# A four-layer attention and feed-forward kernel: three job tables reordered, one table load moved, 16-bit reads in the last layer's quantiser

## The reference, cut to what matters

```
x = x + L0_xattn(layernorm(x), ctx)      # cross attention, 8 heads of 64          "l0x"
x = x + L0_ffn(layernorm(x))             # causal attention, 16 heads of 64 ("l0f"), then 31 + 1 experts ("l0m")
x = x + L1_xattn(layernorm(x), ctx)      # cross attention, 16 heads of 8          "l1x"
x = x + L1_ffn(layernorm(x))             # causal attention, 16 heads of 8 ("l1f"), then 8 experts ("l1m")
x = x + L2_xattn(...);  x = x + L2_ffn(...)                # "l2x", "l2m"
x = x + L3_xattn(...);  x = x + L3_ffn(layernorm(x))       # "l3x", "l3m"
```

```
x    = act_qdq(x)                          # scale = max|x| / 32767; round, clip, times scale
up   = act_qdq(x @ w_up.T);  gate = act_qdq(x @ w_gate.T)
sig  = fixed_qdq_u16(sigmoid(gate))        # steps of 1/65536
gate = act_qdq(gate * sig);  o = act_qdq(gate * up);  return o @ w_down.T
```

## Time and profile before

| | |
|---|---|
| median of 3 runs | 1324.61 us (1323.27 to 1331.3) |
| the profiled execution | 1321.66 us, its span 1319.8 us |
| granted TensorE clock, mean over the span | 0.961 of full speed |
| PE busy | 1160.2 us, 88% of the span |
| DVE busy | 995.9 us, 75% |
| ACT busy | 875.7 us, 66% |
| POOL busy | 560.5 us, 42% |
| the chain that ended last | PE 59%, ACT 17%, DVE 14%, issue 7% |
| ACT exponentials L1096 on that chain | 13% |

### The profile page before, as it was taken

One profiled execution on the slowest core, in us unless ns is written; L12 is line 12 of the kernel. 1 busy time (PEld: TensorE's weight loads), 2 busy tenths in 40 slices (PEclk: granted clock), 3 DMA queues, 4 the chain that ended last, 5 costly groups with the idle time before them and its releaser, 6 DMA issues.

```text
span 1319.8 us, 29320 instructions
## 1 busy us (share of the span) xinstructions
PE 1160.2 (88%) x10082; PEld 894.7 (68%) x10082; DVE 995.9 (75%) x2234; ACT 875.7 (66%) x2403; POOL 560.5 (42%) x670
## 2 busy tenths in 40 slices
PE   7889889999988999997888899988999989997815
PEld 4677777788766788885666677766788666666403
DVE  6676677667758899997777766767666787887787
ACT  4666466656654799995888777764566447775684
POOL 5710366766653222255222231132877417881100
PEclk8999999999998999997999999998999899998967
DMA  5230000000002556650000010003222028750001
GB/s 168 60 93 16 20 2 2 2 3 2 2 2 87 181 210 212 209 208 1 2 2 2 3 42 2 2 2 114 88 88 84 0 55 206 190 139 1 1 0 33
DMA packets 38865, 83.71 MB, mean 63 GB/s; under 512 B 6066, under 2 KB 19762, under 8 KB 38740
## 3 DMA queue, kind: packets, MB, share of 16 engines
q1 hardware_dynamic: 38740, 82.07, 20.2%
HBM read 80.40 MB, written 1.64 MB: 62 GB/s over the span
## 4 chain that ended last, share of the span: by engine, by line
PE 59%; ACT 17%; DVE 14%; issue 7%; POOL 2%; DMA 1%; ACTq 0%; SPq 0%; POOLq 0%; DVEq 0%
PE score_bank L1662 18%; ACT h_all L1096 13%; PE f_bank L1696 6%; PE score_bank L1521 6%; PE f_bank L1422 4%; PE turn_bank L1537 4%; PE turn_bank L1696 3%; PE out_bank L1696 3%; PE out_bank L1577 2%; PE out_bank L1546 2%; DVE top_score L2006 2%; PE f_bank L1447 1%; DVE work L2018 1%; PE f_bank L1454 1%; DVE part_max L2404 1%
## 5 line engine op out<-in xcount | busy, mean ns | idle before, releaser
L1096 ACT ACTIVATE h_all<-score_bank,top_score 128x128 f32<-128x128 f32 x896 | 276.6, 400 | 101.3 <-DVE top_score L2006 101.2
L1662 PE MATMUL score_bank<-parts 128*128 128x512 f32 x1040 | 296.4, 403 | 9.8 <-DVE h_parts L2212 6.6
L1662 PEld LDWEIGHTS score_bank<-parts 128*128 128x128 f32 x1040 | 191.9, 190 | 75.2 <-DVE h_parts L2212 19.0
L2006 DVE TENSOR_REDUCE top_score<-score_bank 128x4 f32<-128x512 f32 x224 | 143.1, 681 | 105.2 <-PE score_bank L1521 105.2
L2212 DVE TENSOR_TENSOR h_parts<-score_bank,h_parts 128x512 fp32r<-128x512 f32 x260 | 178.3, 686 | 2.7 <-ACT h_parts L1211 2.4
L1211 ACT ACTIVATE h_parts<-score_bank 128x512 fp32r<-128x512 f32 x260 | 155.5, 598 | 31.8 <-PE f_bank L1696 8.5
L778 POOL TENSOR_TENSOR small<-small,half_neg 128x4 f32<-128x4 f32 (+4 forms) x24 | 36.6, 1528 | 177.0 <-DVE small L1981 83.2
L1537 PE MATMUL turn_bank<-CF,h_all 128*128 128x128 f32 x512 | 81.7, 283 | 30.3 <-DVE work L2018 19.0
L1537 PEld LDWEIGHTS turn_bank<-CF,h_all 128*128 128x128 f32 x512 | 56.1, 142 | 57.1 <-POOL h_all L803 18.1
L1188 ACT ACTIVATE score_bank<-score_bank,wset 128x512 f32<-128x512 f32 x128 | 84.6, 662 | 11.8 <-PE score_bank L1662 7.0
L2184 DVE TENSOR_TENSOR score_bank<-work,score_bank 128x512 f32<-128x512 f32 x124 | 86.3, 696 | 8.2 <-ACT score_bank L1188 5.6
(11 more groups left out here) (417 smaller groups left out, 2623.6 us busy)
## 6 DMA issues: line engine op xcount, KB each, us to landing
work<-gates_l0m SPq DMA_DIRECT2D x62, 512.0 KB, 3.9
W0X<-gates_l2m SPq DMA_DIRECT2D x32, 256.0 KB, 3.9
CTX<-gates_l2m SPq DMA_DIRECT2D x32, 256.0 KB, 3.9
wset<-in_l0m SPq DMA_DIRECT2D x32, 128.5 KB, 3.6
W0X<-gates_l1m SPq DMA_DIRECT2D x8, 512.0 KB, 3.8
wset<-in_l1m SPq DMA_DIRECT2D x8, 384.0 KB, 4.6
CTX<-gates_l1m SPq DMA_DIRECT2D x6, 512.0 KB, 4.0
big<-in_w0f SPq DMA_DIRECT2D x4, 512.0 KB, 3.9
```

Of the source, the lines that this page charges most:

```text
L1096: last = act.activation(held[c][:, P * m:P * m + P], score_bank[c][:, P * m:P * m + P], ACT.Exp, bias=top_score[c][:, m:m + 1], **sums)
L1662: last = pe_.matmul(bk[:, :], wt, y[:, x], start=(part == 0), stop=(part == len(parts_of) - 1))
L2006: dve.tensor_reduce(top_score[c][:, :], split(score_bank[c][:, :], HEADS), AX_X, ALU.max, negate=True)\
```

## The change

1. In l0x, DVE's C0 of the last batch goes ahead of N0 of the own batch.
2. In l1x and l1f, three jobs each are moved one place back: on ACT SP goes behind E1, on PE OB goes behind T1, on DVE OB goes behind C1.
3. In S of the causal stages the matmul of two columns (L1498) is taken out, 32 in all.
4. In l3m, `gate_steps` and `other` are taken out, six instructions each. The sigmoid, the product with the sigmoid and the final product now read the low 16 bits of the rounded float32 values in place, through a view as int16 with a stride of two (`steps_in`). The order of roundings, copies and sigmoids on ACT changes with that.
5. A sigmoid of one column ahead of l3m's first wait on ACT makes the table load come there.
6. One POOL wait at the start of l1f uses l1x's number of front jobs in its count instead of l1f's, and the memset of `less_magic` goes.

```diff
@@ ORDER, one line of each list as an example
-        DVE=[("M", 0, "own"), ("M", 1, "own"), ("CS", 0, "next"), ("OP", 0, "before"), ("N", 0, "own"), ("C", 0, "last"), ("C", 1, "last"),
+        DVE=[("M", 0, "own"), ("M", 1, "own"), ("CS", 0, "next"), ("OP", 0, "before"), ("C", 0, "last"), ("N", 0, "own"),
...
-        ACT=[("F", 0, "next"), ("E", 0, "own"), ("SP", 0, "last"), ("E", 1, "own"), ("E", 2, "own"), ("E", 3, "own"),
+        ACT=[("F", 0, "next"), ("E", 0, "own"), ("E", 1, "own"), ("SP", 0, "last"), ("E", 2, "own"), ("E", 3, "own"),
...
+        def steps_in(t, at):
+
+            h = HIDDEN_ORDER[at]
+            return t[:, 1024 * h:1024 * h + 1024].bitcast(I16).rearrange("p (n two) -> p n two", two=2)[:, :, 0]
...
-                                r, k = place(front_at["l1x"], L["front"], PAIRS - 1, s, 0)
+                                r, k = place(front_at["l1x"], LAYERS[2]["front"], PAIRS - 1, s, 0)
...
-            pool.memset(less_magic[:, :], -MAGIC)
...
+            act.activation(prob_rec[0][:, 0:1], top_score[0][:, 0:1], ACT.Sigmoid)
+
             act.wait_ge(step("l3m.scale"), 1)
...
             def sigmoid(at):
-                act.wait_ge(step("l3m.g"), at + 1)
+                act.wait_ge(step("l3m.g_round"), at + 1)
                 if at >= 2:
                     act.wait_ge(step("l3m.gs"), at - 1)
-                act.activation(sig[at % 2][:, :], piece(big, at), ACT.Sigmoid, scale=quant[:, 2, 2:3]).then_inc(step("l3m.sig"), 1)
-
-            def other(at):
-
-                act.wait_ge(step("l3m.u_round"), at + 1)
-                act.activation(piece(U, at), piece(U, at), ACT.Identity, bias=less_magic[:, :]).then_inc(step("l3m.u"), 1)
+                act.activation(sig[at % 2][:, :], steps_in(big, at), ACT.Sigmoid, scale=quant[:, 2, 2:3]).then_inc(step("l3m.sig"), 1)
...
                 rounded(big, at, 2, "l3m.g_round")
-                if at < 3:
-                    copies(0, at + 1)
-                if at == 4:
-                    act.wait_ge(step("l3m.scale"), 3)
-                if at >= 4:
-                    rounded(U, at - 4, 1, "l3m.u_round")
+                if 0 < at < 4:
+                    copies(0, at)
                 sigmoid(at)
-            for at in range(2, 6):
+            act.wait_ge(step("l3m.scale"), 3)
+            for at in range(3):
                 rounded(U, at, 1, "l3m.u_round")
-            for at in range(2):
-                other(at)
             act.wait_ge(step("l3m.scale"), 4)
             for at in range(6):
                 rounded(big, at, 3, "l3m.round3")
-                if 1 <= at <= 4:
-                    other(at + 1)
+                if at < 3:
+                    rounded(U, at + 3, 1, "l3m.u_round")
...
                         if causal:
-
-                            pe_.matmul(banks[0][:, 0:2], ident_bf, own_bf[:, 0:2], start=True, stop=True, skip_group_check=True)
...
-            def gate_steps(at):
-                dve.wait_ge(step("l3m.g_round"), at + 1)
-                dve.tensor_scalar(piece(big, at), piece(big, at), MAGIC, None, ALU.subtract).then_inc(step("l3m.g"), 1)
-
             def by_sigmoid(at):
...
-                dve.scalar_tensor_tensor(piece(big, at), sg, MAGIC / 65536.0, piece(big, at), ALU.subtract, ALU.mult)\
+                dve.scalar_tensor_tensor(piece(big, at), sg, MAGIC / 65536.0, steps_in(big, at), ALU.subtract, ALU.mult)\
...
             chunk_max(0, 0)
-            gate_steps(0)
-            chunk_max(0, 1)
             for at in range(6):
-                if at < 5:
-                    gate_steps(at + 1)
                 last = by_sigmoid(at)
-                if at < 2:
-                    others = chunk_max(0, at + 2)
-                if at == 1:
+                if at < 3:
+                    others = chunk_max(0, at + 1)
+                if at == 2:
                     join_max(others, 1, slice(0, 12))
-                if at == 2:
+                if at == 3:
                     scale(1, 2)
...
-                dve.wait_ge(step("l3m.u"), at + 1)
-                dve.scalar_tensor_tensor(piece(big, at), piece(big, at), MAGIC, piece(work, at), ALU.subtract, ALU.mult)\
+                dve.wait_ge(step("l3m.u_round"), at + 1)
+                dve.scalar_tensor_tensor(piece(big, at), piece(big, at), MAGIC, steps_in(work, at), ALU.subtract, ALU.mult)\
```

More of the change, by code:

```diff
@@ L15 @@
 U8 = mybir.dt.uint8
+I16 = mybir.dt.int16
 P = 128
@@ L54 @@
              ("F", 3, "next")],
-        DVE=[("M", 0, "own"), ("M", 1, "own"), ("CS", 0, "next"), ("OP", 0, "before"), ("N", 0, "own"), ("C", 0, "last"), ("C", 1, "last"),
-             ("N", 1, "own"), ("Y", 0, "after")],
+        DVE=[("M", 0, "own"), ("M", 1, "own"), ("CS", 0, "next"), ("OP", 0, "before"), ("C", 0, "last"), ("N", 0, "own"),
+             ("C", 1, "last"), ("N", 1, "own"), ("Y", 0, "after")],
         POOL=[]),
@@ L70 @@
         PE=[("S", 0, "own"), ("OP", 0, "before"), ("F", 1, "next"), ("V", 0, "last"), ("V", 1, "last"), ("V", 2, "last"),
-            ("V", 3, "last"), ("F", 2, "next"), ("T", 0, "own"), ("OB", 0, "last"), ("T", 1, "own"), ("F", 3, "next"),
+            ("V", 3, "last"), ("F", 2, "next"), ("T", 0, "own"), ("T", 1, "own"), ("OB", 0, "last"), ("F", 3, "next"),
             ("F", 0, "after"), ("T", 2, "own"), ("OT", 0, "last"), ("T", 3, "own")],
-        ACT=[("F", 0, "next"), ("E", 0, "own"), ("SP", 0, "last"), ("E", 1, "own"), ("F", 1, "next"), ("E", 2, "own"),
+        ACT=[("F", 0, "next"), ("E", 0, "own"), ("E", 1, "own"), ("SP", 0, "last"), ("F", 1, "next"), ("E", 2, "own"),
              ("E", 3, "own"), ("F", 3, "next"), ("OT", 0, "last"), ("C", 3, "own")],
         DVE=[("M", 0, "own"), ("OP", 0, "before"), ("M", 1, "own"), ("M", 2, "own"), ("M", 3, "own"), ("F", 2, "next"),
-             ("C", 0, "own"), ("OB", 0, "last"), ("C", 1, "own"), ("C", 2, "own")],
+             ("C", 0, "own"), ("C", 1, "own"), ("OB", 0, "last"), ("C", 2, "own")],
         POOL=[("Y", 0, "after")]),
@@ L79 @@
         PE=[("S", 0, "own"), ("OP", 0, "before"), ("F", 1, "next"), ("V", 0, "last"), ("V", 1, "last"), ("V", 2, "last"),
-            ("V", 3, "last"), ("F", 2, "next"), ("T", 0, "own"), ("OB", 0, "last"), ("T", 1, "own"),
+            ("V", 3, "last"), ("F", 2, "next"), ("T", 0, "own"), ("T", 1, "own"), ("OB", 0, "last"),
             ("F", 0, "after"), ("T", 2, "own"), ("OT", 0, "last"), ("T", 3, "own")],
-        ACT=[("F", 0, "next"), ("E", 0, "own"), ("SP", 0, "last"), ("E", 1, "own"), ("E", 2, "own"), ("E", 3, "own"),
+        ACT=[("F", 0, "next"), ("E", 0, "own"), ("E", 1, "own"), ("SP", 0, "last"), ("E", 2, "own"), ("E", 3, "own"),
              ("C", 2, "own"), ("OT", 0, "last"), ("C", 3, "own")],
         DVE=[("M", 0, "own"), ("OP", 0, "before"), ("M", 1, "own"), ("M", 2, "own"), ("M", 3, "own"), ("F", 1, "next"),
-             ("C", 0, "own"), ("OB", 0, "last"), ("F", 2, "next"), ("C", 1, "own")],
+             ("C", 0, "own"), ("C", 1, "own"), ("OB", 0, "last"), ("F", 2, "next")],
         POOL=[("Y", 0, "after")]),
@@ L269, in build @@
         quant = sb("quant", [P, 6, 4])
-        less_magic = sb("less_magic", [P, 1])
         part_max = sb("part_max", [P, 24])
```

## The result

The changed kernel took 1311.68 us (median of 11 runs, 1308.70 to 1316.98), the kernel before 1323.27 (11 runs of that series, 1321.90 to 1331.30): a ratio of 0.9905, 95% interval 0.9888 to 0.9923. That is 11.6 us by medians; the forecast was 1309 us, range 1303 to 1316. The profiled execution took 1309.09 us with a span of 1307.3, 12.5 us less than before's 1319.8. The prediction had 15.2 us. The interval of the ratio lies on both sides of 0.99, so a gain of over 1%, to which the prediction gave 0.60, is neither shown nor excluded; a gain as such is clear.

The account below looks back on a forecast made before the run. No engine was full; a chain of waits bound the kernel. Terms 5.3 + 3.0 + 1.3 + 5.2 + 0.4 = 15.2 us off the profiled 1321.66 gave 1306.5, plus 2.95 to the median, 1309 us; range 1303 to 1316.

Parts of the forecast that it names:

- the two orders with the matmul: Heads of 8 rows: 5.3 us in l1f and 3.0 in l1x from the orders, 1.3 from the matmul.
- the first case: Whole kernel: everything goes as reckoned, 1306 to 1312 us; chance 0.56.
- The exponentials ahead of SP: l1x and l1f on ACT: E1 ahead of SP removes ACT's wait, 0.35 us per l1f batch, 0.23 per l1x batch.
- The two-column matmul: S on PE: removing it gives 0.09 us per l1f batch, 1.3 us for 15 batches; nothing taken in l0f.
- the first reading: l1f on PE: without the two columns the mask matmuls start 0.58 us behind T3 instead of 0.67.
- rival 2: PE's tiling-mode drain decides: removing the matmul costs 0.05 us in all 32 places, total 1312.3 us; chance 0.13.
- rival 3: l1x and l1f: OB becomes what T3 waits for, eating up to all 8.3 us, 1311 to 1317.7; chance 0.15.
- l3m: Last layer: DVE's unbroken stretch lasts 24.24 us and the joined maximum ends at 1279.7, not 1284.87: 5.2 us gained.
- Rivals 4 and 5: l3m's strided 16-bit reads slow: half rate, 1322.0 us, chance 0.05; or a third of the rate, 1335, chance 0.03.
- the whole phase moves as it is: l3m's final products: ACT's roundings keep ahead of DVE by 0.1 us a piece, so phase and output keep their length.
- l0x: C0 ahead of N0: +0.9 beside POOL's cast, +0.6 at the join, -1.1 one step later; 0.4 us, between -3 and +2.

Follow-up runs that it names:

- e1: The kernel before with only the changed l1x and l1f orders on ACT, PE and DVE, two-column matmul kept; ratio to before 0.9936.
- e8: The kernel before with only ScalarE's order changed in l1x and l1f; one execution, span 1313.7 us, l1f 8.00 and l1x 8.07 us a batch.
- e9: The kernel before with only the PE and DVE orders changed in l1x and l1f; one execution, span 1327.2 us.
- e2: The kernel before with only l3m's gate part changed (16-bit reads, no subtractions), table load left with the first sigmoid; ratio 0.9963.
- e6: The changed kernel without its early one-column sigmoid, so the table loads at the first real sigmoid; 1309.50 us, ratio to before 0.9885.
- e4: The changed kernel with DVE's old order kept for the last step of l0x; 1306.74 us, ratio to before 0.9867.
- e12: The changed kernel with DVE's old order in the last step of l0x, run a second time; 1308.30 us, ratio to before 0.9873.
- e11: The changed kernel a third time, no edit; one execution, span 1306.7 us.
- e10: The changed kernel without the early table load and without six filler matmuls behind PE's gap in the last layer; one execution, span 1305.1 us.

## Why the prediction was right, point by point

Of the forecast's 15.2 us, the two orders with the matmul had 9.6, and the l1x and l1f batches behind the first got shorter by 9.1; l3m had 5.2 and got 5.21. The number came out 2.7 us too low by medians, at the slow edge of the first case (1306 to 1312), for a reason that the prediction has no term for: the clock, below.

**The exponentials ahead of SP** were to bring 0.35 us in l1f and 0.23 in l1x. e1 shows 0.34 and 0.22. The pricing was right: what the wait was, less what E1 waits for its maximum. It said nothing on which queue earns it. By e8 and e9, l1f's gain is all ScalarE's; in l1x ScalarE alone gets 0.11, PE and DVE alone lose 0.12, and together there are 0.22.

**The two-column matmul** was taken at 0.09 us in l1f and 0 in l0f. Between e1 and the changed kernel l1f has 0.08, and l0f's period is 14.54 us before and 14.53 after. The mask matmuls start 0.59 us behind T3, as the first reading had it, and the drain (rival 2) did not show as time in either stage.

**OB next** (rival 3) came to the edge and not over it: DVE's OB is done at 813.50, 0.25 us ahead of the last exponentials' end, where 0.3 was forecast. T3 follows OT, which follows DVE's `tmpT`, and no idle time of PE is left ahead of T3. With OB's order untouched l1f had the same 8.00 us (e8), so the new place of OB costs nothing there. Anything more that comes off the exponentials would have to come off OB too.

**l3m**: 24.24 us of DVE's stretch were forecast, 24.24 were measured (1248.11 to 1272.35), and 5.21 us came off for 5.2. The table load counts for 1.28 of them (e2, e6). Reads of 16-bit halves at a stride of two cost nothing on 12 products: 1.22 to 1.23 us each, as before. Rivals 4 and 5 are out. The Trainium skill, "ScalarE: Activation LUTs", What ACT_TABLE_LOAD costs, has a drain of 1380 ns on top of the load; no row here shows it: with the load late, it starts 0.02 us behind the rounding's end and the sigmoid 0.02 us behind its own (e2), and moving it off the path was worth 1.28 us, not 2.66. The final phase, the prediction's "the whole phase moves as it is", did so: from the joined maximum to the end of the span 34.97 us before and 34.95 after.

**l0x** was the weak term: 0.4 us by +0.9, +0.6 and -1.1. The loss behind the join was sized right: 1.07 us by e4, 1.1 forecast; the 0.6 ahead of it came to 0.41 (21.12 before, 20.71 without the loss). But the 0.9 was no property of the order. The kernels with the old order had the long batch beside POOL's cast twice (before and e9, 9.10 us, the cast 2.2 us into the batch) and twice not (e1, e2, 8.20 us, 2.5 us into it or more); e8, with the old order too and the cast at 2.4, had 10.92, but with the clock at half from 72.6 to 76.0 us, and says nothing. Those with the new one had 8.19 to 8.25, with the cast at 2.4 or later. What sets the cast's place was not looked into, and whether the new order helps at 2.2 was not seen: that 0.9 us is in the measured difference, but as luck. Two batches ahead of it got 0.1 us shorter each. The join as a whole lost 0.66 us, the steady batches kept 7.97.

**What was missing** is TensorE's clock at the stages' ends. Read from the two profiled spans, with the sign of after less before:

| stretch | us | of it clock |
|---|---|---|
| to the last l0f batch | -0.20 | |
| l0m, to the first l1x batch | -0.43 | -0.43 |
| first l1x period (7.34 for 8.34) | -1.00 | -1.00 |
| the other l1x and l1f batches | -9.10 | |
| l1m to the last normalisation | +0.52 | not told apart, see below |
| last normalisation to first scaled tokens | +2.89 | +2.9 |
| gate's scale to the joined maximum | -5.21 | |
| the rest | +0.03 | |
| sum | -12.50 | +1.46 |

The l0m stretch has nothing of the change in it and took 233.6 to 239.9 us in these executions; the one from l1m to the last normalisation, also outside the change, 356.0 to 361.3, so its +0.52 is within what one kernel does. What lies in the change comes to 14.0 us (12.5 + 1.46), or 14.5 if the half microsecond between l1m and the last normalisation is the clock's too, against 15.2 forecast. The first l1x period shows the same thing with the other sign: in the changed kernel's profile the clock rose at 618 us and not at 625, and that period was 7.34 us. In e1 to e9 and e12 it was 8.29 to 8.33, new tables or old, and 8.43 in e11; only e10, whose clock rose at 617 us, had 7.33 as well. So that microsecond was luck. Taking one profiled execution as the base made the forecast blind to both. What it left out is that the part of l3m ahead of the gate could change its length: it put the early load into ACT's wait of 3.94 us, where it did fit, and for PE's gap beside that wait it has no term at all. The prediction's total was right because the priced steps were, and because 2.9 us lost to the clock here met 1.4 us won by it elsewhere and a range 13 us wide.

## What to carry to other kernels

A job that waits for another engine, with ready work queued behind it, is priced well by its idle time less the next job's own wait; check the queues of the other engines for the same job, since half of the gain can hang on them (l1x: 0.11 of 0.22 us). Where a per-batch order is changed, look at the join with the next stage by itself: there the same move cost 1.07 us, and keeping the old order for that one step won it back. Fillers that keep a clock up must stand in the gap in which it can fall, not behind it; behind it they make the fall dearer. And list the falls of the clock in both profiles before giving a difference of two spans to the change.

## What the runs showed of the hardware

The same kernel's span goes with its mean granted clock: seven runs of the kernel before on one chip lay between 1314.9 us at 0.968 and 1328.7 at 0.955. A gap of 2.38 us on PE, the same in all of them, saw a fall to 1.2 GHz in seven of twelve executions, 1.5 to 1.7 us after PE went idle, and no fall in the two in which fillers stood in it; after a fall the clock stayed at half for 3.4 or 6.8 us. A sigmoid over 1024 int16 halves of float32 words takes 1.15 us in four of the six pieces and 1.17 to 1.20 in the other two; over float32 it took 1.13 to 1.15.
